# A Haar-wavelet convolution block on one core: a new order of VectorE's work in the head, moved steps around the last image, and GpSimd adding x for the first halves of five tail slots

## The chip, the cores and the metric

One NeuronCore of one Trainium2 chip runs the whole program. The metric is the device time of one execution in microseconds, median of several runs; lower is better.

## What is computed

For each of 8 images of 256 channels and 160x160 pixels, with all channels mixed by 1x1 convolutions:

```python
ll, lh, hl, hh = haar_dwt(x)                                   # 80x80 each
wav = concatenate([ll, lh, hl, hh], axis=1)                    # 1024 channels
fused = relu(bn_eval(conv1x1(wav, fusion_w, fusion_b), ...))   # 256 channels
sp_in = concatenate([mean(fused, 1), max(fused, 1)], axis=1)   # two maps
spatial_out = sigmoid(conv7x7(sp_in, sa_w)) * fused
ch_map = sigmoid(mlp(mean(spatial_out, (2, 3))) + mlp(max(spatial_out, (2, 3))))
projected = relu(bn_eval(conv1x1(ch_map * spatial_out, proj_w, proj_b), ...))   # 1024 channels
return haar_idwt(projected) + x
```

So an image's projection can't start before its fusion is complete, its two maps are convolved, the sigmoid has gated all of it, and the pooled channels have gone through the small network.

## The kernel before

**Tiles and slots.** An image is cut into 14 tiles of 6 or 5 rows of the 80x80 grid (480 or 400 pixels; 6,6,6,6,6,5,5 twice), 112 tiles in all. The program is a row of 133 slots. Slot k runs stage A (fusion) for tile k, while there is one, and stage C (projection, inverse Haar, add x, store) for tile kc = k - 21. Slots 0 to 20 have only A (the head), slots 112 to 132 only C (the tail). In the code `s.a` and `s.c` say which stages a slot has, `s.kn` is the next slot's kc, and `s.phase` is the slot's place (0 to 7) in what an image needs between its last fusion tile and its first projection tile:

- phase 0: the per-pixel sums and maxima over channels, collected in `blocksum` and `blockmax`, are turned by four TensorE transposes (`across_psum`), reduced by VectorE (`spatial_maps`) and sent through DRAM (`map_scratch`) to `maps`.
- phase 1: TensorE convolves (`convolve`, 28 matmuls), ScalarE takes the sigmoid, SP stores it (`sig_scratch`).
- phases 2 to 5: VectorE multiplies two chunks of 800 pixels a slot into `fused` (`gate`, four instructions at L896, `GATED`). The factors come by DMA, chunk by chunk, alternately into `sigb` and a piece of `xre`; for the last image all of them come in two DMAs into `x_lo` and `x_hi`. In the next slot ScalarE sums the same chunks (`chunk_means`).
- phase 6 (`LAST - 1`): VectorE pools (`pool_chunks`), TensorE multiplies by `squeeze`; phase 7 (`LAST`): `excite_channels`, the factors `ch`, and the first tile of C.

Slots 14 to 21 are phases 0 to 7 of the first image, slots 112 to 119 those of the last.

**Stage A of one tile** has two halves i (128 channels each). For each half: DMA to `xin`; ScalarE rounds to `x_hi` (`x_upper`, L633) once TensorE has read the previous tile's half; VectorE takes the rest, `x_lo = xin - x_hi` (`x_lower`, L777); TensorE runs 24 matmuls (`fusion`, L570). After both halves ScalarE writes `fused` (L725). For each tile GpSimd adds the two channel halves (`channel_sum`, L447) and VectorE takes their maximum, transposes both and reduces (`turn`, L913, L927, L932). In slots 1 to 11 VectorE also builds the matrices of the 7x7 convolution (`bands`, L832, L836).

**Stage C of one tile**: ScalarE and VectorE/GpSimd split y into `y_hi` and `y_lo` (L902 on VectorE, `lower` L462 on GpSimd), TensorE runs 24 matmuls for each half (`project`, L542), ScalarE and VectorE take relu and butterflies (L666, L861, L863), and VectorE writes the output pixels (`cells`, L880). x is added in one of two ways, which `adding(kc, i)` chooses: true, the cells go to `xre` and GpSimd issues a DMA that adds x from DRAM to them (L454); false, SP loads x to `xre` (`load_residual`, L351), the cells go to `xin`, and GpSimd adds them with four TENSOR_TENSORs (`sum_x`, L472). SP then stores `xre`.

**What sets the order.** Each engine's queue is written out by hand: `body(s)` of every engine is called slot after slot, and the engines meet in semaphores. What is written behind a waiting instruction on its engine waits too. SP is the queue of nearly all loads and stores.

In the head VectorE's `body` is, in this order: `x_lower(k+1, 0)`, `x_lower(k+1, 1)` (from slot 3 on), `turn`, first chunk's `gate`, `spatial_maps`, `bands`, second chunk's `gate`.

Of the kernel before, what the change touches and what calls it, by code (L numbers as in the profile page):

```python
# [11 lines left out]
P = 128  # L12
# [31 lines left out]
def haar_block(nc, x, fusion_w, fusion_b, bn1_g, bn1_b, bn1_m, bn1_v, sa_w, ca_w1, ca_w2,  # L44
# [47 lines left out]
    with ExitStack() as ctx:  # L92
# [191 lines left out]
        def adding(kc, i):  # L284

            return kc + LAG < NT or 2 <= kc + LAG - NT < LAST
# [33 lines left out]
        def _(sp):  # L320
# [46 lines left out]

            def store_sig(s):
# [4 lines left out]
            def body(s):  # L373
# [53 lines left out]
        def _(gp):  # L427
# [10 lines left out]
            def channel_sum(s):  # L438
# [5 lines left out]
                if s.load_next:  # L444
                    gp.wait_ge(xlo_ready[0], s.k + 2)
# [54 lines left out]
        def _(pe):  # L500
# [85 lines left out]

            def body(s):
                if s.a:
                    fusion(s, 0)
                if s.phase == LAST and not s.a:  # L590
                    excite_channels(s)
# [7 lines left out]
                if s.phase == 0:  # L599
                    pe.wait_ge(mlp_ready, 2)  # L600
                    pe.wait_ge(blockmax_ready, s.k)
                    pe.wait_ge(blocksum_ready, s.k)
                    for to, blocks in ((across_sum, blocksum), (across, blockmax)):
                        for h in range(2):
                            n = NPX // GROUP // 2
                            mm = pe.transpose(to[:, h * P:(h + 1) * P], blocks[:, h * n:(h + 1) * n], ident[:, :])
                    mm.then_inc(across_psum, 1)
# [5 lines left out]
                if s.c:  # L613
                    project(s, 1)
                if s.phase == 1 and not s.a:
                    convolve(s)
                if s.phase == LAST - 1:
                    pe.wait_ge(pool_ready, 2 * (s.nb + 1))
                    for i in range(CT):
                        mm = pe.matmul(squeezed, squeeze[:, i, :], pool[:, i, :], start=(i == 0), stop=(i == CT - 1))  # L620
# [408 lines left out]
```

## Time and profile before

| | |
|---|---|
| median of 3 runs | 2400.68 us (2397.55 to 2400.82) |
| the profiled execution, its own time | 2394.07 us |
| its span in the trace | 2392.3 us |
| TensorE busy | 2303.3 us (96%) |
| VectorE busy | 2065.7 us (86%) |
| ScalarE busy | 1137.2 us (48%) |
| GpSimd busy | 584.9 us (24%) |

The busy shares are means over a head, a long middle and a tail that differ; the rows further down take them apart. In the rows PE is TensorE, DVE VectorE, ACT ScalarE, POOL GpSimd and SPq the DMA issues of SP's queue.

### The profile page before, as it was taken

How to read it: one execution, taken by the hardware profiler on the slowest of the kernel's cores; microseconds unless marked ns; L12 is line 12 of the kernel's file. 1: busy time of each engine (PE TensorE's matmuls, PEld its weight loads, DVE VectorE, ACT ScalarE, POOL GpSimd, SP SyncE). 2: the span in 40 equal slices, each digit the busy share in tenths (PEclk: the TensorE clock that was granted, in tenths of full speed). 3: DMA queues.
4: the chain of work that ended last, by engine and by line, in shares of the span. 5: the costliest groups of instructions: out<-in, count | busy, mean ns of one | idle time of the engine just before them, and what ended most of it. 6: DMA issues, size and time to landing. Idle time of an engine off the chain costs nothing. (4 is left out here: it accounts for less than half of the span.)

```text
span 2392.3 us, 30200 instructions
## 1 busy us (share of the span) xinstructions
PE 2303.3 (96%) x11109; PEld 2039.9 (85%) x11109; DVE 2065.7 (86%) x2571; ACT 1137.2 (48%) x1535; POOL 584.9 (24%) x549
## 2 busy tenths in 40 slices
PE   7998799999999999999999999999999999998897
PEld 6886689888898988989899898988889898886786
DVE  6885688898888988899888989889888898889899
ACT  4443544465444554455444564446544464434433
POOL 0110122122221221211222112212212112133698
PEclk9999899999999999999999999999999999999999
DMA  5454499999999999999999999999999999989998
GB/s 188 168 183 147 151 277 283 278 310 284 294 286 295 288 286 288 288 281 306 282 277 297 293 307 281 283 278 297 295 293 283 283 307 280 280 238 286 346 354 324
DMA packets 112759, 660.54 MB, mean 276 GB/s; under 512 B 17698, under 2 KB 18788, under 8 KB 112356
## 3 DMA queue, kind: packets, MB, share of 16 engines
q1 hardware_dynamic: 84964, 479.04, 51.8%
q0 software_dynamic: 27648, 179.58, 39.2%
q8 instruction: 87, 1.43, 0.2%
q14 instruction: 60, 0.49, 0.1%
HBM read 448.24 MB, written 210.33 MB: 275 GB/s over the span
## 5 line engine op out<-in xcount | busy, mean ns | idle before, releaser
L542 PE MATMUL pp<-y_hi,wp_hi 128*128 128x480 f32 (+1 forms) x1792 | 670.5, 374 | 24.8 <-DVE sd L863 11.7
L633 ACT ACTIVATE x_hi<-xin 128x1920 fp32r<-128x1920 f32 (+1 forms) x224 | 418.7, 1869 | 542.9 <-PE pfs L570 461.0
L542 PE MATMUL pp<-y_lo,wp_hi 128*128 128x480 f32 (+1 forms) x1792 | 666.1, 372 | 0.0
L542 PE MATMUL pp<-y_hi,wp_lo 128*128 128x480 f32 (+1 forms) x1792 | 664.1, 371 | 0.0
L777 DVE TENSOR_TENSOR x_lo<-xin,x_hi 128x1920 fp32r<-128x1920 f32 (+1 forms) x224 | 461.5, 2060 | 214.1 <-ACT x_hi L633 213.1
L570 PE MATMUL pfs<-x_hi,wf_hi 128*128 128x480 f32 (+1 forms) x1648 | 616.4, 374 | 13.7 <-DVE x_lo L777 13.3
L570 PE MATMUL pfs<-x_lo,wf_hi 128*128 128x480 f32 (+1 forms) x1648 | 614.3, 373 | 0.0
L570 PE MATMUL pfs<-x_hi,wf_lo 128*128 128x480 f32 (+1 forms) x1648 | 614.2, 373 | 0.0
L666 ACT ACTIVATE relu<-pp,t 128x480 f32<-128x480 f32 (+1 forms) x448 | 285.6, 639 | 351.6 <-PE pp L542 351.2
L880 DVE SCALAR_TENSOR_TENSOR xre<-sd,both 128x960 f32<-128x960 f32 (+1 forms) x364 | 410.2, 1169 | 6.1
L542 PEld LDWEIGHTS pp<-y_hi,wp_hi 128*128 128x128 f32 x1792 | 338.2, 189 | 76.0 <-DVE sd L863 15.5
L542 PEld LDWEIGHTS pp<-y_hi,wp_lo 128*128 128x128 f32 x1792 | 337.9, 189 | 40.7
L542 PEld LDWEIGHTS pp<-y_lo,wp_hi 128*128 128x128 f32 x1792 | 337.8, 189 | 38.5
L454 POOL DMA_DIRECT2D xre<-in_x_dram x192 | 170.0, 885 | 800.0 <-DVE xre L880 800.0
L570 PEld LDWEIGHTS pfs<-x_hi,wf_hi 128*128 128x128 f32 x1648 | 311.5, 189 | 53.7 <-DVE x_lo L777 15.4
L570 PEld LDWEIGHTS pfs<-x_hi,wf_lo 128*128 128x128 f32 x1648 | 312.0, 189 | 36.7
L570 PEld LDWEIGHTS pfs<-x_lo,wf_hi 128*128 128x128 f32 x1648 | 311.4, 189 | 36.6
L861 DVE SCALAR_TENSOR_TENSOR sd<-pp,nbias,relu 128x480 f32<-128x480 f32 (+1 forms) x406 | 278.9, 687 | 53.3 <-PE pp L542 30.0
L863 DVE SCALAR_TENSOR_TENSOR sd<-pp,nbias,relu 128x480 f32<-128x480 f32 (+1 forms) x406 | 277.7, 684 | 0.0
L447 POOL TENSOR_TENSOR xre<-fused 128x480 f32<-128x480 f32 (+2 forms) x112 | 136.2, 1216 | 511.8 <-issue 258.2
L725 ACT ACTIVATE fused<-pfs,t 128x480 f32<-128x480 f32 (+1 forms) x206 | 129.2, 643 | 256.9 <-PE pfs L570 256.9
L462 POOL TENSOR_TENSOR y_lo<-y_full,y_hi 128x480 fp32r<-128x480 f32 (+1 forms) x112 | 134.2, 1198 | 472.9 <-DVE x_lo L777 410.4
(105 smaller groups left out, 1595.5 us busy)
## 6 DMA issues: line engine op xcount, KB each, us to landing
xin<-in_x_dram SPq DMA_DIRECT2D x160, 960.0 KB, 7.8
out_dram<-xre SPq DMA_DIRECT2D x160, 960.0 KB, 7.5
xre<-in_x_dram POOLq DMA_DIRECT2D x136, 960.0 KB, 10.3
xin<-in_x_dram SPq DMA_DIRECT2D x64, 800.0 KB, 7.3
out_dram<-xre SPq DMA_DIRECT2D x63, 800.0 KB, 5.9
xre<-in_x_dram POOLq DMA_DIRECT2D x56, 800.0 KB, 9.5
xre<-in_x_dram SPq DMA_DIRECT2D x24, 960.0 KB, 7.0
sigb<-sig_scratch SPq DMA_DIRECT2D x28, 400.0 KB, 8.5
```

What stands on the lines that cost most here:

```text
L447: nc.gpsimd.tensor_tensor(stats[:, 0:n], fused[:, 0, here], fused[:, 1, here], ALU.add).then_inc(sm_ready, 1)
L454: nc.gpsimd.dma_start(xre[:, home[g], 0:4 * px_of(kc)], dram(x_v, kc, i), accum_op=ALU.add).then_inc(x_added[home[g]], 16)
L462: nc.gpsimd.tensor_tensor(y_lo[:, kc % 2, 1, 0:n_px], y_full[:, 0:n_px], y_hi[:, kc % 2, 1, 0:n_px].bitcast(F32), ALU.subtract).then_inc(l ...
L542: mm = pe.matmul(pp[j][:, 0:n_px], w[:, kt, cols], y[:, s.pc, kt, 0:n_px], start=(kt == 0 and m == 0), stop=(kt == CT - 1 and m == 2))
L570: mm = pe.matmul(bank(s.k, o)[:, 0:n_px].rearrange("p (y w) -> p y w", w=W2), w[:, i, q, o * P:(o + 1) * P], v[:, q % 2, :, q // 2, :], st ...
L633: nc.scalar.activation(halves(x_hi, i, k), pairs(i, k), ACT.Copy).then_inc(xhi_ready[i], 1)
L666: nc.scalar.activation(relu[:, n, 0:n_px], pp[j][:, 0:n_px], ACT.Relu, bias=bias2[:, j * CT + i:j * CT + i + 1]).then_inc(r_ready, 1)
L725: nc.scalar.activation(fused[:, o, ring(s.k)], bank(s.k, o)[:, 0:px_of(s.k)], ACT.Relu, bias=bias1[:, o:o + 1]).then_inc(f_ready, 1)
L777: nc.vector.tensor_tensor(halves(x_lo, i, k), pairs(i, k), halves(x_hi, i, k).bitcast(F32), ALU.subtract).then_inc(xlo_ready[i], 1)
L861: nc.vector.scalar_tensor_tensor(rows[:, :, 0, :], p, low, q, ALU.max, ALU.add).then_inc(sd_ready, 1)
L863: nc.vector.scalar_tensor_tensor(rows[:, :, 1, :], p, low, q, ALU.max, ALU.subtract).then_inc(sd_ready, 1)
L880: nc.vector.scalar_tensor_tensor(px[:, :, :, c], s0, both[:, c, i:i + 1], s1, ALU.add, op).then_inc(cell_ready, 1)
```

## The change

No arithmetic changes. (1) In all head slots VectorE runs `head_body`: `turn` first, then `x_lower(k+1, 0)`, pooling, both chunks' gates, `spatial_maps`, `bands`, and `x_lower(k+1, 1)` last. (2) GpSimd's `channel_sum` no longer waits for `x_lower` in the head. (3) In slot 112 the four transposes stand behind `project(s, 1)` instead of ahead of it, `spatial_maps` behind `cells(s, 1)`, and SP stores the maps behind a store and a load. (4) In slot 118 the two small matmul groups stand inside `project(s, 1)`, the small relu ahead of the half's last relu, and `lower` of the next tile ahead of `cells(s, 1)`. (5) `adding` is false for the first halves of slots 114 to 118: SP loads x and GpSimd adds it there.

```diff
-            return kc + LAG < NT or 2 <= kc + LAG - NT < LAST
+            return kc + LAG < NT or i == 1 and 2 <= kc + LAG - NT < LAST
...
-                if s.phase == 0:
-                    sp.wait_ge(across_ready, 2 * (s.nb + 1))
-                    for m in range(2):
-                        sp.dma_start(map_dram[m:m + 1, :].rearrange("o (h p j) -> (o p) h j", h=2, j=GROUP),
-                                     across_all[:, m, :, :]).then_inc(map_stored, 16)
+                if s.phase == 0 and s.a:
+                    store_maps(s)
...
                 if s.c_next and not adding(s.kn, 1):
                     load_residual(s.kn, 1)
+                if s.phase == 0 and not s.a:
+                    store_maps(s)
...
                 gp.wait_ge(f_ready, CT * (k + 1))
-                if s.load_next:
+                if s.load_next and s.c:
                     gp.wait_ge(xlo_ready[0], s.k + 2)
...
                 for n, j in enumerate((LH, LL, HH, HL)):
+                    if s.phase == LAST - 1 and not s.a and i == 1:
+                        if n == 2:
+                            squeeze_channels(s)
+                        if n == 3:
+                            excite_channels(s)
...
                 for n, j in enumerate((LH, HH)):
+                    if n == 1 and i == 1 and s.phase == LAST - 1 and not s.a:
+                        hidden(s)
...
+            def head_body(s):
+
+                if s.turn:
+                    turn(s)
+                x_lower(s.k + 1, 0)
+                if s.phase == LAST - 1:
+                    pool_chunks(s)
+                if s.phase in GATED:
+                    for hand in range(2):
+                        gate(s, GATED[s.phase][hand])
+                if s.phase == 0:
+                    spatial_maps(s)
+                bands(s)
+                x_lower(s.k + 1, 1)
+                if s.c_next:
+                    lower(s.kn)
...
-                if s.c:
-                    butterflies(s, 1)
-                    cells(s, 1)
-                bands(s)
+                butterflies(s, 1)
+                if s.phase == LAST - 1 and not s.a:
+                    lower(s.kn)
+                cells(s, 1)
+                if s.phase == 0 and not s.a:
+                    spatial_maps(s)
```

VectorE's queue in a head slot with gates (slot 17), before; `x_lo` rows are `x_lower`, ISA rows the gate's instructions and their accumulator reads:

```order
L777 TENSOR_TENSOR x_lo<-xin,x_hi 128x1920 x2
L913 TENSOR_TENSOR xre<-fused 128x480
L927 STREAM_TRANSPOSE sd<-xre 128x960
L932 TENSOR_REDUCE blocksum<-sd 128x15
L932 TENSOR_REDUCE blockmax<-sd 128x15
L896 ISA fused,part<-fused,sigb 128x800
L896 ISA part 128x1
L896 ISA fused,part<-fused,sigb 128x800
L896 ISA part 128x1
L896 ISA fused,part<-fused,xre 128x800
L896 ISA part 128x1
L896 ISA fused,part<-fused,xre 128x800
```

The same place in the changed kernel:

```order
L955 TENSOR_REDUCE blockmax<-sd 128x15
L800 TENSOR_TENSOR x_lo<-xin,x_hi 128x1920
L919 ISA fused,part<-fused,sigb 128x800
L919 ISA part 128x1
L919 ISA fused,part<-fused,sigb 128x800
L919 ISA part 128x1
L919 ISA fused,part<-fused,xre 128x800
L919 ISA part 128x1
L919 ISA fused,part<-fused,xre 128x800
L919 ISA part 128x1
L800 TENSOR_TENSOR x_lo<-xin,x_hi 128x1920
L936 TENSOR_TENSOR xre<-fused 128x480
```

Turn and gates (four instructions, each with a read) stood behind both `x_lo` of their slot; now the turn stands ahead of both, and the gates between the two.

SP's queue in slots 112 and 113, before (`xre<-in_x_dram` are `load_residual`, `out_dram<-xre` stores):

```order
L351 DMA xre<-in_x_dram 128x1920
L391 DMA map_scratch<-sigb 100x2x32 x2
L359 DMA out_dram<-xre 128x1920
L351 DMA xre<-in_x_dram 128x1920
L402 DMA maps<-map_scratch 80x2x80
L359 DMA out_dram<-xre 128x1920 x2
L371 DMA sig_scratch<-sig 80x80
```

And in the changed kernel:

```order
L352 DMA xre<-in_x_dram 128x1920
L360 DMA out_dram<-xre 128x1920
L352 DMA xre<-in_x_dram 128x1920
L372 DMA map_scratch<-sigb 100x2x32 x2
L408 DMA maps<-map_scratch 80x2x80
L360 DMA out_dram<-xre 128x1920
L352 DMA xre<-in_x_dram 128x1920
L360 DMA out_dram<-xre 128x1920
L378 DMA sig_scratch<-sig 80x80
```

The map stores moved behind one store and one load of 960 KB, and slot 113 has a load more, for slot 114's first half.

GpSimd's queue over slots 114 to 116, before (`xre<-in_x_dram` is the adding DMA):

```order
L462 TENSOR_TENSOR y_lo<-y_full,y_hi 128x480
L454 DMA xre<-in_x_dram 128x1920 x2
L462 TENSOR_TENSOR y_lo<-y_full,y_hi 128x480
L454 DMA xre<-in_x_dram 128x1920 x2
L462 TENSOR_TENSOR y_lo<-y_full,y_hi 128x400
```

And in the changed kernel:

```order
L468 TENSOR_TENSOR y_lo<-y_full,y_hi 128x480
L478 TENSOR_TENSOR xre<-xre,xin 128x480 x4
L460 DMA xre<-in_x_dram 128x1920
L468 TENSOR_TENSOR y_lo<-y_full,y_hi 128x480
L478 TENSOR_TENSOR xre<-xre,xin 128x480 x4
L460 DMA xre<-in_x_dram 128x1920
L468 TENSOR_TENSOR y_lo<-y_full,y_hi 128x400
```

In each slot one adding DMA became four tensor instructions, which stand behind the slot's `cells(s, 0)`, that is beside VectorE's `y_lo` and first gate chunk.

## Rows read from the trace of the kernel before

**Rows 1.** The page, its first line.

```profile
span 2392.3 us, 30200 instructions
```

**Rows 2.** Stretches: length, busy time and instructions of each engine, granted clock, DMA share, GB/s.

```profile
20.00:182.00 162.00, 154.43 (x735) 134.87 (x734) 127.49 (x202) 72.00 (x64) 18.94 (x14) 1.00 0.48 169
182.00:300.00 118.00, 92.61 (x427) 80.33 (x426) 71.34 (x87) 58.96 (x78) 11.58 (x10) 0.90 0.43 149
300.00:2120.00 1820.00, 1818.64 (x8855) 1620.92 (x8854) 1608.21 (x1924) 891.52 (x1200) 369.59 (x360) 1.00 0.98 288
...
2169.00:2229.00 60.00, 44.37 (x210) 36.98 (x209) 59.58 (x94) 32.39 (x64) 12.89 (x14) 0.98 1.03 285
```

**Rows 3.** TensorE's waits, 20 to 182.5 us: total, times, longest.

```profile
PE pp L570 <- DVE x_lo L777: 4.4, 4, 1.8
PE pfs L570 <- DVE x_lo L777: 3.0, 3, 1.8
```

**Rows 4.** TensorE's waits, 182.5 to 300 us.

```profile
PE pfs L570 <- DVE x_lo L777: 10.3, 2, 5.6
PE pm L606 <- DVE blockmax L932: 7.1, 1, 7.1
PE pm L620 <- DVE pool L950: 4.9, 1, 4.9
PE pp L570 <- DVE x_lo L777: 3.0, 1, 3.0
```

**Rows 5.** Timeline of VectorE, slot 2 to 3: start, duration.

```profile
58.19 0.65 DVE L913 TENSOR_TENSOR xre<-fused 128x480 f32<-128x480 f32 x1
...
61.27 0.76 DVE L832 TENSOR_SCALAR band<-relu 80x80 f32<-80x80 f32 x4
...
63.36 2.15 DVE L777 TENSOR_TENSOR x_lo<-xin,x_hi 128x1920 fp32r<-128x1920 f32 x1
```

**Rows 6.** Timeline of ScalarE and VectorE, gates of slot 16, start of 17.

```profile
223.85 0.84 ACT L677 ACTIVATE pm<-fused 128x800 f32<-128x800 f32 x1 [6.03 <-DVE part L896]
...
225.72 1.91 ACT L633 ACTIVATE x_hi<-xin 128x1920 fp32r<-128x1920 f32 x1
...
227.66 2.16 DVE L777 TENSOR_TENSOR x_lo<-xin,x_hi 128x1920 fp32r<-128x1920 f32 x1 [2.02 <-ACT x_hi L633]
```

**Rows 7.** Timeline of VectorE and GpSimd, slots 5 and 6.

```profile
85.07 3.67 DVE L777 TENSOR_TENSOR x_lo<-xin,x_hi 128x1600 fp32r<-128x1600 f32 x2
87.02 2.81 POOL L447 TENSOR_TENSOR xre<-fused 128x480 f32<-128x480 f32 x1 [9.71 <-DVE x_lo L777]
88.66 1.68 DVE L913 TENSOR_TENSOR xre<-fused 128x480 f32<-128x480 f32 x1
```

**Rows 8.** DMA issues, 205 to 300 us: KB, median us to landing.

```profile
sigb<-sig_scratch SPq DMA_DIRECT2D x4, 400.0 KB, 4.1
...
sig_scratch<-sig SPq DMA_DIRECT2D x1, 25.0 KB, 4.2
```

**Rows 9.** The page, DMA issues of the whole run.

```profile
sigb<-sig_scratch SPq DMA_DIRECT2D x28, 400.0 KB, 8.5
```

**Rows 10.** Timeline of SP's queue and TensorE, slots 112 and 113.

```profile
2135.82 0.64 PE L606 MATMUL pm<-ident,blocksum 128*100 128x128 f32 x2 [5.34 <-DVE blockmax L932]
...
2146.54 0.80 SPq L391 DMA_DIRECT2D map_scratch<-sigb  x2
...
2156.86 2.63 PE L583 MATMUL pm<-maps,band 80*80 80x80 f32 x28 [2.15 <-DMA maps<-map_scratch]
```

**Rows 11.** Groups of GpSimd's instructions, 2120 to 2393 us: busy, mean ns.

```profile
L472 POOL TENSOR_TENSOR xre<-xre,xin 128x480 f32<-128x480 f32 (+1 forms) x124 | 145.4, 1209 | 15.3 <-DVE xin L880 12.8 <-DMA xre<-in_x_dram 2.5
```

**Rows 12.** Timeline of VectorE and GpSimd, second gates of slot 116.

```profile
2205.88 0.98 DVE L896 CUSTOM_DVE_ANT_0 fused<-fused,x_hi 128x800 f32<-128x800 f32 x1
...
2206.28 1.48 POOL L462 TENSOR_TENSOR y_lo<-y_full,y_hi 128x400 fp32r<-128x400 f32 x1
```

**Rows 13.** Timeline of GpSimd and TensorE, slots 118 to 119.

```profile
2227.59 1.19 POOL L462 TENSOR_TENSOR y_lo<-y_full,y_hi 128x480 fp32r<-128x480 f32 x1 [2.63 <-ACT y_hi L693]
...
2229.36 0.77 PE L542 MATMUL pp<-y_hi,wp_hi 128*128 128x480 f32 x1 [4.02 <-DVE y_lo L902]
```

More of the change, by code:

```diff
@@ L366, in load_sig, with store_maps @@
                              ).then_inc(sigb_landed[c % 2], 16)
+            def store_maps(s):
+                sp.wait_ge(across_ready, 2 * (s.nb + 1))
+                for m in range(2):
+                    sp.dma_start(map_dram[m:m + 1, :].rearrange("o (h p j) -> (o p) h j", h=2, j=GROUP),
+                                 across_all[:, m, :, :]).then_inc(map_stored, 16)
             def store_sig(s):
@@ L585, in convolve, with gather, squeeze_channels @@
                 mm.then_inc(conv_psum, 1)
+            def gather(s):
+                pe.wait_ge(mlp_ready, 2)
+                pe.wait_ge(blockmax_ready, s.k)
+                pe.wait_ge(blocksum_ready, s.k)
+                for to, blocks in ((across_sum, blocksum), (across, blockmax)):
+                    for h in range(2):
+                        n = NPX // GROUP // 2
+                        mm = pe.transpose(to[:, h * P:(h + 1) * P], blocks[:, h * n:(h + 1) * n], ident[:, :])
+                mm.then_inc(across_psum, 1)
+            def squeeze_channels(s):
+                pe.wait_ge(pool_ready, 2 * (s.nb + 1))
+                for i in range(CT):
+                    mm = pe.matmul(squeezed, squeeze[:, i, :], pool[:, i, :], start=(i == 0), stop=(i == CT - 1))
+                mm.then_inc(hid_psum, 1)
             def body(s):
@@ L598, in body @@
                     fusion(s, 1)
[L599 to L607, printed above, removed]
+                if s.phase == 0 and s.a:
+                    gather(s)
                 if s.phase == 1 and s.a:
@@ L614, in body @@
                     project(s, 1)
+                if s.phase == 0 and not s.a:
+                    gather(s)
                 if s.phase == 1 and not s.a:
                     convolve(s)
[L617 to L620, printed above, removed]
-                    mm.then_inc(hid_psum, 1)
+                if s.phase == LAST - 1 and s.a:
+                    squeeze_channels(s)
             body(slots[0])
@@ L950, in pool_chunks @@
                 nc.vector.tensor_reduce(pool[:, :, 1], part[:, 1, :, :], AX.X, ALU.max).then_inc(pool_ready, 1)
+            def head_body(s):
[13 more added lines that the diff above has]
+                    lower(s.kn)
             def body(s):
-                ahead = s.phase == LAST
+                if not s.c:
+                    head_body(s)
+                    return
                 if s.load_next:
                     x_lower(s.k + 1, 0)
-                if s.load_next and other(s.k) != other(s.k + 1):
-                    x_lower(s.k + 1, 1)
-                if ahead and not s.a:
-                    lower(s.kc)
-                if s.c:
-                    butterflies(s, 0)
-                    if s.phase == 0:
-                        turn(s)
-                    if s.phase == LAST - 1:
-                        pool_chunks(s)
-                    cells(s, 0)
+                butterflies(s, 0)
+                if s.phase == 0:
+                    turn(s)
+                if s.phase == LAST - 1:
+                    pool_chunks(s)
+                cells(s, 0)
                 if s.c_next and not s.next_is_first:
                     lower(s.kn)
-                if s.phase == LAST - 1 and not s.c:
-                    pool_chunks(s)
-                if s.turn and not (s.phase == 0 and s.c):
+                if s.turn and s.phase != 0:
                     turn(s)
@@ L974, in body @@
                     gate(s, GATED[s.phase][0])
-                if s.load_next and other(s.k) == other(s.k + 1):
+                if s.load_next:
                     x_lower(s.k + 1, 1)
-                if s.phase == 0:
+                if s.phase == 0 and s.a:
                     spatial_maps(s)
@@ L980, in body @@
                     lower(s.kn)
-                if s.c:
-                    butterflies(s, 1)
-                    cells(s, 1)
-                bands(s)
+                butterflies(s, 1)
+                if s.phase == LAST - 1 and not s.a:
+                    lower(s.kn)
+                cells(s, 1)
+                if s.phase == 0 and not s.a:
+                    spatial_maps(s)
                 if s.phase in GATED:
```

10 lines of the change are left out of this document (5 added, 5 removed).

## The prediction

> **What bounds the kernel now.** I read three views: the stretches, TensorE's waits, and the timelines around those waits. From 300 to 2120 us TensorE is busy 1818.6 of 1820 us [rows 2]: nothing but less TensorE work helps there, the change leaves every queue of those slots as it is, and a gain in the head therefore passes through it in full. The idle time is at both ends. From 20 to 182 us TensorE waits 4.4 + 3.0 = 7.4 us in seven places for VectorE's `x_lo` [rows 3]. From 182.5 to 300 it waits 10.3 + 7.1 + 4.9 + 3.0 = 25.3 us, always for VectorE [rows 4], at a granted clock of 0.90 [rows 2]: part of that stretch ran at 1.2 GHz, after waits of 5 to 7 us. The middle takes 1818.6 / 8855 = 0.205 us for a TensorE instruction, the stretch 182 to 300 has 427 of them, so 88 us of work took 92.6: about 5 us more are the clock's. From 2169 to 2229 us (slots 114 to 118) VectorE is busy 59.6 of 60 us and TensorE 44.4 [rows 2]: VectorE is the bound there, and whatever delays it is paid in full.
>
> **Slots 1 to 13.** A 480-pixel half of fusion is 24 matmuls of about 0.216 us (0.205 scaled to 6 rows), 5.2 us; a 400-pixel half 4.3. Between two halves run ScalarE's `x_hi`, 1.9 us [rows 6], and VectorE's `x_lo`, 2.1 us [rows 5]: 4.1 us with the handovers, so a half has 1.1 us to spare. VectorE's turn takes 61.27 - 58.19 = 3.1 us and the matrices 63.36 - 61.27 = 2.1 [rows 5]. Before, both stand in one gap between two `x_lo`, 5.2 us where 3.1 are free and 1.1 to spare: 1 us of wait a slot, and the seven waits are this. After, each gap holds one of the two. The turn alone still meets GpSimd's `channel_sum`, which now asks for SBUF just as `x_lo` ends. How such a meeting goes is seen once: GpSimd's sum took 2.81 us beside two `x_lo`, and VectorE's maximum behind them 1.68 instead of the 0.65 of [rows 5], until GpSimd was done [rows 7]. I count the turn at 3.1 + 1.1 = 4.2 us. VectorE's slot is then 2 x 2.1 + 4.2 + 2.2 = 10.6 against TensorE's 10.4: 0.1 to 0.2 us of wait in ten slots, 1.3 in all, and in the two pairs of 400-pixel slots, where TensorE needs only 8.6, about 1 us each. Left 3.3, **gain 4.1** (bounds 2 and 7.4).
>
> **Slots 14 to 20.** The turn of tile 13 now stands ahead of the transposes' need, so the 7.1 us wait goes. What replaces the others I follow in time, 0 being the end of slot 14's fusion. Fusion 15 runs 0.7 to 11.1, the convolution (2.6 us, [rows 10]) to 13.7. The sigmoid's store is issued at 16 (ScalarE's `x_hi`, relus and sigmoid), lands 4.2 later, the gate rows 4.1 after that [rows 8]: 24.3. VectorE has slot 16's first `x_lo` done by 23, waits for the rows, gates two chunks (four instructions of 0.98 overlapping to 0.91, [rows 12]) to 28.0, lets GpSimd's sum pass (1.2, [rows 11]), and has the second `x_lo` at 31.3, where TensorE wanted it at 29.3: 2.0 us of wait. From there VectorE's slot is turn, `x_lo`, gates 3.7, `x_lo`, that is 3.1 to 4.2 + 2.1 + 3.7 + 2.1 = 11 to 12 us, against TensorE's 10.4 (slots 17 and 18) and 8.6 (19 and 20). It gives waits of 0.1 and 0.5 in slot 17 to 18, 0.8 and 2.4 in 19, 0.6 and 1.2 in 20, and 2.2 ahead of the pooled matmul, which comes at 71.9. Sum 9.8. The decisive point is what no longer happens: ScalarE's `x_hi` at 225.72 stood behind a chunk sum that had waited 6.03 us for a gate, VectorE's `x_lo` then waited 2.02 for `x_hi` [rows 6], and TensorE for that. Now the gates of a slot are done before ScalarE asks for them in the next. Waits 25.3 - 9.8 = 15.5, and with no wait above 2.4 us most of the clock's 5 us, I say 4: **gain 19.5** (bounds 12 and 25).
>
> **Slot 112.** TensorE's 5.34 us wait for `blockmax` goes, since the transposes stand behind `project(s, 1)`. But the wait behind it grows. The convolution waited for the maps until 2156.86, and SP issued their stores only at 2146.54 [rows 10], although the transposes came at 2135.82: SP's queue stood behind a store's landing, which this change does not touch. Now one store and one load of 960 KB go ahead of the map stores too. Issue time for both is 0.8 us; their bytes take 3.4 us each at the 285 GB/s of [rows 2], but they were ahead of the load of the maps before as well, so I take 1.1 us of them: **loss 1.9**. Bounds: a gain of 7.4 if both waits vanish (5.3 + 2.1), a loss of 7.6 if all bytes come on top.
>
> **Slots 114 to 117, GpSimd's adds.** Four adds of 1.21 us [rows 11] start as `cells(s, 0)` ends, beside `y_lo` and the first chunk's two gate instructions. DMA gets lighter (share 1.03), but VectorE is the bound, and no wait on a DMA stands there. By the pattern of [rows 7] VectorE's next two-input instruction goes first, then GpSimd's and VectorE's alternate: `y_lo`, add, gate, add, gate, and the last two adds lie beside the butterflies. So two adds are paid a slot: three 480-pixel slots x 2.4 and one of 400 pixels x 2.0 = **loss 9.3**. The bounds: 0, if a gate never waits for GpSimd (none was seen to; [rows 12] show only GpSimd's `y_lo` stretched to 1.48 beside a gate of the usual 0.98), and 4 x 4.84 = 19.4, if every add is paid. I take the value between, as [rows 7] is the nearest case of VectorE waiting.
>
> The Trainium skill (SBUF — State Buffer, Who interferes with whom) says that a VectorE instruction with two SBUF inputs and a GpSimd instruction that reads SBUF exclude each other for the whole instruction, whoever starts first. [Rows 7] and [rows 12] agree, one for each direction. By the page alone this term is the loss just given, by [rows 12] alone it could be 0; the sum above keeps its value without the page.
>
> **Slot 118.** Before, GpSimd's `y_lo` waited 2.63 us for ScalarE and TensorE restarted at 2229.36 after 4.02 us [rows 13]. The moved matmuls let ScalarE finish the channel factors some 2 us sooner, but GpSimd now has four 400-pixel adds (4.1 us) ahead of that `y_lo`, and TensorE needs both halves of y. The two cancel: loss 0.5. With a lighter DMA the first residual of slot 119 lands sooner, for a gain of 1.2 of GpSimd's wait (2.5, [rows 11]). **Gain 0.7** (bounds: gain 4.0, the whole wait; loss 4.8, the whole adds).
>
> **Sum.** -4.1 - 19.5 + 1.9 + 9.3 - 0.7 = -13.1. Span 2392.3 [rows 1] to 2379.2. Beside the span the profiled execution has 1.8 us, so 2381.0; it ran 6.6 us under the median of the three runs, and against that median the prediction is 2400.7 - 13.1 = **2387.6**. Its own range, with 5 us either way in the head and 4 in the tail, is 2381 to 2394.
>
> **Rivals.**
> A, the gates are not held up by GpSimd. Speaks for it: no gate of before is seen stretched; against: hardly any met a running GpSimd instruction first. Without the 9.3 it is 2378.3.
> B, every add is paid, because GpSimd wins each boundary, `y_lo` and second-chunk gates included: 10.1 more, 2397.7, no change. For it: VectorE has no slack at all; against: two adds lie beside butterflies and cells, which read PSUM.
> C, slower. In the head `x_lower(k+1, 1)` is now queued behind gates that wait for a DMA. If the gate rows land as in the middle of the run, 8.5 us [rows 9], and not 4.1, each of four slots pays 4.4 more, 17.6: 2405.2. It decides from a landing of about 7.4 us on (13.1 / 4 = 3.3 more). For it: VectorE keeps its order whatever is late, and TensorE has 1.1 us to spare; against: the head's DMA share is 0.43 [rows 2], and the landings of just these loads are the 4.1.
> D, slot 112 gives its 5.3 and 2.1 us after all: 2378.3 as well.
>
> **From these to the numbers.** Likeliest case 0.52, A or D or a head better than counted 0.24, B or a head worse than counted 0.17, C 0.07. What can be told from no change is 0.2%, 4.8 us: 2395.9 to 2405.5. The likeliest case and A, D lie below it, B and a weak head about there, C at its upper edge or over it. Faster 0.82, same 0.13, slower 0.05. The range 2376 to 2397 takes in A, D and most of B.
>
> **What the changed profile would show.** Right: no wait for `blockmax` near 182 us, waits before 182 us of 3 us in all, none over 3 us up to 300, granted clock there 0.97 or more, ScalarE's chunk sums waiting for no gate; in slot 112 a longer wait for the maps, 8 to 11 us; in slots 114 to 117 one or two gate instructions a slot at 2 us instead of 0.98, and those slots 2 us longer each. Wrong: gates at 0.98 throughout there (A), `y_lo` and four gates stretched (B), or `x_lo` late behind idle VectorE time that a gate load ends (C).

## The result and the profile after

The changed kernel takes **2374.66 us** (median of 4 runs, 2371.9 to 2376.96), the kernel before 2399.11 beside it: ratio 0.9899, interval 0.9882 to 0.9917. That is 24.4 us faster, where 13.1 were forecast, and 1.3 us below the low end of the range. Timed again on another occasion (e7) it was 2375.05 against 2398.44, ratio 0.9905 (0.989 to 0.992). The profiled execution took 2376.96 us, the slowest of its four; that of the kernel before had been faster than any of the runs beside it. So the two first traces differ by only 17.3 us, and further traces of both were taken (e7, e8, e13, e14).

The stretches of the changed kernel, columns as in [rows 2]:

```profile
20.00:182.00 162.00, 159.94 (x764) 139.94 (x763) 144.50 (x210) 75.27 (x67) 28.25 (x15) 1.00 0.50 175
182.00:300.00 118.00, 111.95 (x541) 96.03 (x540) 99.29 (x112) 69.21 (x90) 20.48 (x16) 1.00 0.67 216
300.00:2120.00 1820.00, 1814.78 (x8839) 1616.59 (x8837) 1608.38 (x1931) 890.98 (x1204) 379.31 (x367) 1.00 0.98 287
2120.00:2169.00 49.00, 33.68 (x140) 28.62 (x141) 34.71 (x44) 15.04 (x28) 25.76 (x19) 0.79 0.88 301
```

In the second row TensorE does 541 instructions in the time of 427 [rows 2], at a granted clock of 1.00 for 0.90. The middle is full as before. The fourth row holds about slots 113 to 115: at a granted clock of 0.79 the convolution's 28 matmuls take 4.02 us behind a wait of 8.79, where they took 2.63 behind 2.15 [rows 10]. TensorE's waits, 20 to 182.5 us (two rows) and 182.5 to 300 us (three):

```profile
PE pp L581 <- DVE x_lo L800: 1.1, 2, 0.8
PE pfs L581 <- DVE x_lo L800: 0.8, 1, 0.8
...
PE pp L581 <- DVE x_lo L800: 3.5, 3, 1.8
PE pfs L581 <- DVE x_lo L800: 1.8, 2, 1.6
PE pm L612 <- DVE pool L973: 0.4, 1, 0.4
```

That is 1.9 us for the 7.4 of [rows 3], and 5.7 for the 25.3 of [rows 4]; the wait for `blockmax` is gone. Now the tail. SP's queue and TensorE in slots 112 and 113, the places of [rows 10]:

```profile
2116.03 1.74 SPq L372 DMA_DIRECT2D map_scratch<-sigb  x2
2126.29 0.31 SPq L408 DMA_DIRECT2D maps<-map_scratch  x1
2128.12 2.16 PE L594 MATMUL pm<-maps,band 80*80 80x80 f32 x14 [8.79 <-DMA maps<-map_scratch]
```

VectorE and GpSimd in slots 114 and 116, then GpSimd and TensorE in slots 118 to 119 ([rows 12, 13]):

```profile
2144.36 1.68 DVE L919 CUSTOM_DVE_ANT_0 fused<-fused,x_lo 128x800 f32<-128x800 f32 x1 [1.44 <-DMA x_lo<-sig_scratch]
2145.97 1.97 DVE L919 CUSTOM_DVE_ANT_0 fused<-fused,x_lo 128x800 f32<-128x800 f32 x1
...
2175.77 0.63 DVE L925 SCALAR_TENSOR_TENSOR y_lo<-fused,ch,y_hi 128x400 fp32r<-128x400 f32 x1
2175.99 6.46 POOL L478 TENSOR_TENSOR xre<-xre,xin 128x480 f32<-128x480 f32 x4 [2.73 <-DVE xin L903]
2176.31 2.01 DVE L919 CUSTOM_DVE_ANT_0 fused<-fused,x_hi 128x800 f32<-128x800 f32 x1
2178.25 1.97 DVE L919 CUSTOM_DVE_ANT_0 fused<-fused,x_hi 128x800 f32<-128x800 f32 x1
...
2205.65 4.44 POOL L478 TENSOR_TENSOR xre<-xre,xin 128x400 f32<-128x400 f32 x4 [4.95 <-DVE xin L903]
2210.05 1.20 POOL L468 TENSOR_TENSOR y_lo<-y_full,y_hi 128x480 fp32r<-128x480 f32 x1
2211.35 0.74 PE L553 MATMUL pp<-y_hi,wp_hi 128*128 128x480 f32 x1 [4.28 <-issue]
```

Two gate instructions take 2.01 and 1.97 us instead of 0.98, the four adds 6.46 us instead of 4.8: each gate lets one add pass, and the last two adds end behind the gates, beside the butterflies. In slot 118 the four adds stand ahead of `y_lo`, and TensorE restarts right behind it.

### The profile page after: what moved, and what is told of

The parts are those of the page before. It is cut to its first block and busy times, and to the rows that moved or that the text cites. A ratio compares the mean times of both kernels' runs of the same rounds, so it can differ in the third digit from the quotient of the medians.

```text
span 2375.0 us, 30224 instructions
## 1 busy us (share of the span) xinstructions
PE 2303.4 (97%) x11109; PEld 2038.4 (86%) x11109; DVE 2090.2 (88%) x2571; ACT 1138.7 (48%) x1535; POOL 621.6 (26%) x564
## 5 line engine op out<-in xcount | busy, mean ns | idle before, releaser
L453 POOL TENSOR_TENSOR xre<-fused 128x480 f32<-128x480 f32 (+2 forms) x112 | 147.5, 1317 | 462.3 <-issue 249.0
## 6 DMA issues: line engine op xcount, KB each, us to landing
xre<-in_x_dram POOLq DMA_DIRECT2D x133, 960.0 KB, 10.2
```

The source lines that it names most:

```text
L453: nc.gpsimd.tensor_tensor(stats[:, 0:n], fused[:, 0, here], fused[:, 1, here], ALU.add).then_inc(sm_ready, 1)
```

## The experiments

Four marks cut the run, each the start of an instruction: **mark 23**, the first matmul of slot 23's projection (305.75 us in the first trace of before); **conv**, the first matmul of slot 113's convolution; **restart**, TensorE's first matmul in slot 119; and the end of the span. All times in us.

| run | median (before beside it) | mark 23 | conv less mark | restart less conv | span |
|---|---|---|---|---|---|
| before, first trace | 2400.68 | 305.75 | 1851.1 | 72.5 | 2392.3 |
| e8 before | 2399.36 (2398.44) | 309.44 | 1852.9 | 73.6 | 2399.0 |
| e13 before | one execution, 2396.77 (2398.71) | 307.04 | 1851.8 | 73.2 | 2394.7 |
| e14 before | one execution, 2408.07 (2398.71) | 307.59 | 1853.6 | 73.7 | 2405.1 |
| changed, first trace | 2374.66 (2399.11) | 273.99 | 1854.1 | 83.2 | 2375.0 |
| e7 changed | 2375.05 (2398.44) | 274.25 | 1852.7 | 83.6 | 2374.3 |
| e1 changed, no adds | 2365.43 (2397.97) | 274.49 | 1853.0 | 72.6 | 2365.5 |
| e2 before + adds | 2405.37 (2397.97) | 307.08 | 1849.5 | 81.8 | 2402.6 |
| e3 before + head | 2368.37 (2397.97) | 273.76 | 1856.1 | 74.5 | 2369.9 |
| e4 changed, slot 112 as before | 2372.33 (2397.97) | 275.09 | 1852.3 | 82.4 | 2372.8 |
| e5 head + slot 118 | 2366.16 (2398.44) | 273.74 | 1852.4 | 72.7 | 2364.8 |
| e6 e1 + maps stored first | 2367.38 (2398.44) | 275.48 | 1852.5 | 72.9 | 2367.1 |
| e9 e5, gates behind | 2374.46 (2398.06) | 282.18 | 1852.0 | 72.6 | 2369.2 |
| e10 e5, matrices behind | 2379.84 (2398.06) | 286.76 | 1848.7 | 74.2 | 2373.6 |
| e11 e5, short sum | 2358.44 (2398.06) | 268.00 | 1850.0 | 71.8 | 2355.3 |
| e12 changed, adds in halves | 2373.83 (2398.06) | 274.11 | 1853.7 | 80.2 | 2371.2 |
| e15 e5, sum after maximum | 2369.45 (2398.71) | 278.07 | 1852.0 | 72.8 | 2372.4 |
| e16 e15, turn split | 2363.25 (2398.71) | 273.01 | 1852.7 | 72.8 | 2364.4 |

**e1, the adds undone.**

```diff
-            return kc + LAG < NT or i == 1 and 2 <= kc + LAG - NT < LAST
+            return kc + LAG < NT or 2 <= kc + LAG - NT < LAST
```

> The changed kernel with part 5 undone: in slots 114 to 118 the first halves' x comes by the adding DMA again. My theory (two GpSimd adds are paid a slot, because a gate meets a running add): every gate instruction there is back at 0.98 us, the restart of TensorE in slot 119 comes 9 to 11 us earlier than in the changed kernel (2211.35 there), and the median is 9 to 11 us under the changed kernel's 2374.7, that is 2364 to 2366. Rival (the adds are not what costs; what I read as their price is the slower clock or the later slot 112): gates at 0.98, but the restart within 3 us of 2211 and the median 2372 or more. Second rival (with DMA busy there, the adding DMAs push other transfers late): gates at 0.98 and new waits on DMA of 5 us or more, median about 2370.

Measured 2365.43, ratio 0.9857 (0.9841 to 0.9872), 9.2 us under the changed kernel; the restart came 11.3 us earlier than in its first trace, 0.3 more than expected. The theory held: the gates are back at 0.98, and the second rival's new waits on DMA don't show. Slot 114's gates and the restart:

```profile
2142.26 0.98 DVE L919 CUSTOM_DVE_ANT_0 fused<-fused,x_lo 128x800 f32<-128x800 f32 x1
2143.17 0.99 DVE L919 CUSTOM_DVE_ANT_0 fused<-fused,x_lo 128x800 f32<-128x800 f32 x1
...
2200.08 0.77 PE L553 MATMUL pp<-y_hi,wp_hi 128*128 128x480 f32 x1 [2.72 <-DVE y_lo L925]
```

**e2, the adds alone** (the diff of e1 the other way, in the kernel before).

> The kernel before with part 5 alone: in slots 114 to 118 SP loads x for the first halves and GpSimd adds it. Theory: first-chunk gate instructions take 2.0 us (480-pixel slots) and 1.8 us (400) instead of 0.98, and the whole is 9 to 11 us slower than the kernel before, with no wait on a DMA in it. Rival (gates not held up): 0 to 1 us slower. Rival (the price arises only together with the later transposes of slot 112): under 4 us slower.

Measured 2405.37, ratio 1.0027 (1.0017 to 1.0038): 7.4 us slower, a little under the theory's 9 to 11. Gates of slots 115 to 117 took 2.01, 1.97, 2.00, 1.97, 1.83 and 1.80. One clause was wrong: there is a wait on a DMA.

```profile
2168.03 5.05 POOL L472 TENSOR_TENSOR xre<-xre,xin 128x480 f32<-128x480 f32 x4 [0.35 <-DVE xin L880]
2173.28 0.99 DVE L896 CUSTOM_DVE_ANT_0 fused<-fused,x_lo 128x800 f32<-128x800 f32 x1 [4.78 <-DMA x_lo<-sig_scratch]
2174.20 0.98 DVE L896 CUSTOM_DVE_ANT_0 fused<-fused,x_lo 128x800 f32<-128x800 f32 x1
```

Slot 114's gates wait for their factors, here so long that the adds are over before them; in the changed kernel it is 1.44 us, in e12 2.33. The new load of x for slot 114 stands on SP's queue ahead of the sigmoid's store. From the issue of that store to the load of the factors behind it are 4.2 to 5.6 us in the five traces with this load, and 1.5 to 4.2 in the 13 without it (under 2.6 in ten). That the load delays the factors is read from this; no run has the load without the adds, and in e4, with both, slot 114's gates don't wait.

**e3, the head alone**, in the kernel before (`head_body` as in the change).

```diff
-                if s.load_next:
+                if s.load_next and s.c:
                     gp.wait_ge(xlo_ready[0], s.k + 2)
...
+                if not s.c:
+                    head_body(s)
+                    return
```

> The kernel before with parts 1 and 2 alone, the new order of VectorE's queue in the head and GpSimd's sum without its wait. Theory: the first projection wait of slot 23 comes 30 to 33 us earlier than before (305.75 there), as in the changed kernel (273.99); everything behind it moves as a block, so the median is 30 to 34 us under the kernel before, and together with the 9 to 11 us of the adds and some 2 of slot 112 that makes the 24.4 of the whole change. Rival (the head's gain is the 23.6 of the prediction, and the profiled executions differ by chance): 22 to 26 us in the median, while the slot 23 mark stands at 280 or later.

Measured 2368.37, ratio 0.9871 (0.9854 to 0.9887): 29.6 us faster, mark 23 at 273.76. The rival's 22 to 26 is refuted, the theory's 30 to 34 missed by 0.4. This part alone beats the whole change.

**e4, slot 112 as before; e5, only head and slot 118; e6, part 3 without its later stores.** The core of e4's edit (the same for `gather` and `spatial_maps`):

```diff
-                if s.phase == 0 and s.a:
+                if s.phase == 0:
...
-                if s.phase == 0 and not s.a:
-                    store_maps(s)
```

> The changed kernel with part 3 undone: transposes ahead of project(s, 1), spatial_maps ahead of the cells, the maps' stores ahead of a store and a load. Theory: 1 to 2 us faster than the changed kernel (2372.5 to 2373.7), because TensorE's 5.3 us wait for blockmax comes back but the 8.8 us wait for the maps falls to about 2; the conv starts 1.5 us earlier. Rival (the move itself pays, the stores' place is all that costs): 1 to 3 us slower, the maps wait still over 5 us on top of the 5.3. Rival (no difference): within 1 us, conv start within 0.5 us of 2128.1.

> Head and slot 118 alone: the changed kernel without part 3 (slot 112) and without part 5 (adds). Theory, by addition of what the first runs showed (part 3 costs 2.3 us, the adds 9.2): 2362 to 2364, that is 4 to 6 us under the head alone (2368.4), and TensorE's restart in slot 119 waits 2.7 us instead of 4.8. Rival (part 3 is worth what the difference between e3 and e1 shows, 2.9 us, and slot 118 nothing): 2368 or more.

> The changed kernel without part 5, and with SP's stores of the maps put back ahead of the store and the load in slot 112; the transposes stay behind project(s, 1) and spatial_maps behind the cells. Theory (the landing of small stores behind 960 KB transfers is what part 3 costs): stores are issued about 2115.1 and land about 5.4 us later, not 10; the maps are there 10.3 us after the issue as in the kernel before; the convolution starts at 2125 to 2126 instead of 2127.5 in e1, its wait is 6 to 7 us instead of 8.9, the median 1.5 to 3 us under e1's 2365.4. Rival (the maps share the DMA with the same bytes wherever they stand): conv at 2127 or later, within 1 us of e1.

e4: 2372.33, ratio 0.9887 (0.9872 to 0.9903), some 2.5 us under the changed kernel, 0.2 more than expected. Its waits are those of the theory, 5.34 us for `blockmax` and 2.56 for the maps, though conv comes 0.7 us earlier and not 1.5. But e5 at 2366.16 (ratio 0.9866, 0.9851 to 0.988) isn't below e1, and e6 at 2367.38 (0.9873, 0.9858 to 0.9887) isn't either: both expectations missed, by 2 us or more. The column conv less mark shows why nothing can be told by so little: the traces with the transposes ahead scatter from 1848.7 to 1856.1 there, with waits for the maps from nothing to 7.85 us. In the mean the 13 of them have 1851.9, and the four with the whole of part 3 (both of the changed kernel, e1, e12) 1853.4. e5 is also e3 with part 4: the restart's wait falls from 4.79 to 2.72 us as expected, restart less conv by 1.8, the median by 2.2. The stores in e6, for the three rows above of the changed kernel:

```profile
2116.82 0.80 SPq L372 DMA_DIRECT2D map_scratch<-sigb  x2
2122.37 0.32 SPq L406 DMA_DIRECT2D maps<-map_scratch  x1
2127.98 2.29 PE L592 MATMUL pm<-maps,band 80*80 80x80 f32 x15 [7.80 <-DMA maps<-map_scratch]
```

From issue to the load of the maps it is 5.5 us ahead of the two transfers and 10.3 behind them, as the theory says; but that load then takes 5.6 us instead of 1.8, so the place of 50 KB in the queue shifts the delay and saves 1 us of it. Part 3 costs 0 to 2.5 us by the medians, 1.4 by the means above.

**e7, e8, e13, e14: both kernels traced again,** unchanged.

> The changed kernel once more, so that it is timed on the same chip as these runs. Theory (the first comparison of it was fair, and the 7 us between the difference of the profiled executions, 17.3, and that of the medians, 24.4, come from the profiled execution of before being its fastest and that of the changed kernel its slowest): 23 to 25 us under the kernel before, 2373 to 2376. Rival (the medians were off): 17 to 20 us under it.

> The kernel before once more, with a new trace. Theory: the median is within 2 us of the runs beside it, and this trace, if it is of an execution near the median, shows where 5 to 6 us more are lost than in the first one: waits on DMA in the middle (300 to 2120 us, where the changed kernel has one of 1.04 us) or a lower granted clock at the two ends, 1 us or more each. Rival (nothing differs but the start): the mark of slot 23 within 1 us of 305.75 and the middle within 1 us of 1705.4.

> A third trace of the kernel before. Theory (its head varies by the granted clock behind the waits of 4 to 7 us, not by the waits): TensorE's waits from 182.5 to 300 us sum to 23 to 26 us again, while the slot 23 mark lies anywhere from 305.7 to 310 and goes with the clock of 182 to 300 us: about 306 at 0.90, about 309.5 at 0.84. Rival (the waits themselves vary): the mark over 308 with a clock of 0.90 and waits of 28 us or more.

> A fourth trace of the kernel before. The same expectation as for the third: the mark goes with the clock, not with the waits; over the four traces of before, the head's mean mark is 307 to 309, so that the head's gain is 33 to 35 us and not 31.8.

Mark 23 of the eight traces with the new head (the changed kernel, e1, e3 to e7, e12) lies between 273.7 and 275.5. With the old head it is 305.75, 309.44, 307.04 and 307.59, mean 307.5, as e14's expectation had it; e2, which has the old head too, lies at 307.08. e7's median is 23.4 us under the kernel before, as its theory says. (e14's span is long for another cause too: TensorE waits 5.0 us for `y_lo` at 2286.9, behind the restart, and from the restart to the end it takes 170.2 us where the other three take 162.7 to 163.1.) The stretch 182 to 300 of the old head in e8, e13 and e14:

```profile
182.00:300.00 118.00, 94.62 (x408) 82.57 (x408) 67.73 (x83) 57.67 (x76) 10.32 (x9) 0.84 0.45 149
```

```profile
182.00:300.00 118.00, 92.85 (x423) 80.28 (x422) 70.21 (x86) 58.34 (x77) 10.82 (x9) 0.88 0.44 149
```

```profile
182.00:300.00 118.00, 91.17 (x421) 79.04 (x420) 69.90 (x86) 58.33 (x77) 10.83 (x9) 0.90 0.45 149
```

e8's waits there sum to 23.3 us, less than the 25.3 of [rows 4], and yet its mark is 3.7 us later, with 408 instructions where [rows 2] have 427 and a clock of 0.84: matmuls at 1.2 GHz behind the waits of 4.5 to 7 us. e14 is the other kind: clock 0.90, waits of 26.7 us. So the expectation of e14 (only the clock varies) held for e8 and e13 and not for e14. In e8 the middle took what it took before (TensorE busy 1703.8 of the 1705 us from 310 to 2015, both times), so the waits on DMA there fall.

What the lower clock costs can be read without the waits. Up to mark 23 TensorE does the same 1206 instructions in every one of these traces (e14 records one fewer), so its busy time compares like with like: 259.08 us in the first trace of before, 264.88 in e8, 260.83 in e13, 259.65 in e14, but 252.30 and 252.05 in the two of the changed kernel. First before, then changed, columns as in [rows 2]:

```profile
0.00:305.75 305.75, 259.08 (x1206) 224.90 (x1206) 216.78 (x330) 140.37 (x152) 33.12 (x33) 0.96 0.48 167
...
0.00:273.99 273.99, 252.30 (x1206) 218.77 (x1206) 232.47 (x330) 141.21 (x152) 44.40 (x33) 1.00 0.54 186
```

**e9 and e10, the order inside the head.** In e5's `head_body` the gates, or the matrices, are put behind the second `x_lower`:

```diff
                 x_lower(s.k + 1, 0)
...
-                if s.phase in GATED:
-                    for hand in range(2):
-                        gate(s, GATED[s.phase][hand])
                 if s.phase == 0:
                     spatial_maps(s)
                 bands(s)
                 x_lower(s.k + 1, 1)
+                if s.phase in GATED:
+                    for hand in range(2):
+                        gate(s, GATED[s.phase][hand])
```

> e5 (head and slot 118) with one thing moved: in the head the gates of slots 16 to 19 stand behind x_lower(k+1, 1) instead of ahead of it; the turn stays first, the matrices stay between the x_lower. Theory (the gates' place between the two x_lo is what the gain of slots 14 to 20 rests on): 3.7 us of gates and 3.1 of turn lie in one gap between two x_lo, where 3.1 are free and 1.1 to spare, so 2.5 to 3.5 us of wait in each of four slots, ScalarE's chunk sums wait for gates again, and part of the stretch runs at the lower clock: the slot 23 mark 10 to 16 us later than the 273.7 of e5, the median 2376 to 2382. Rival (the turn's place is what mattered, since it alone took the 7.1 us wait away): the mark within 4 us of 273.7, median under 2370.

> e5 with one thing moved: in the head the matrices (bands) stand behind x_lower(k+1, 1) instead of ahead of it, so that they share a gap with the turn, as they did before the change. Theory (one wait a slot comes from two works in one gap): the waits of TensorE from 20 to 182 us are back at 7 to 9 us instead of 1.9, the slot 23 mark 5 to 8 us later than in e5, median 2371 to 2374. Rival (the gain before 182 us comes from GpSimd's sum no longer waiting for x_lo, and so reaching the turn early): waits stay under 4 us, median within 2 us of e5's 2366.2.

e9: 2374.46, ratio 0.9897 (0.9876 to 0.9919), 8.3 us slower than e5, its mark 8.4 later: below the theory's 10 to 16, above the rival's 4. The rest of the theory shows: ScalarE's chunk sums wait for gates again, 15.2 us in four places, and the granted clock from 182 to 300 us is 0.96. The gates' place is worth 8 us. e10: 2379.84, ratio 0.9925 (0.9906 to 0.9944), mark 13.0 us later where the theory had 5 to 8: its direction held, its size didn't. TensorE's waits, 182.5 to 300 us in e9, then 20 to 182.5 in e10:

```profile
PE pfs L579 <- DVE x_lo L796: 7.8, 2, 4.2
PE pm L610 <- DVE pool L969: 1.8, 1, 1.8
PE pp L579 <- DVE x_lo L796: 1.1, 1, 1.1
```

```profile
PE pp L579 <- DVE x_lo L796: 9.2, 6, 2.8
PE pfs L579 <- DVE x_lo L796: 2.8, 2, 1.9
```

12.0 us in e10 where before the change, with the same two works in one gap, 7.4 stood [rows 3]. The turn isn't longer: its maximum takes 0.65 us there. What GpSimd's sum, freed of its wait, now stretches is the matrices ahead of the turn, whose ten instructions took 2.2 to 2.3 us before:

```profile
112.38 3.17 DVE L855 SCALAR_TENSOR_TENSOR band<-relu,band 80x80 f32<-80x80 f32 x10
115.47 0.64 DVE L932 TENSOR_TENSOR xre<-fused 128x480 f32<-128x480 f32 x1
```

Before, the wait of part 2 kept the sum in VectorE's idle time: from 20 to 182 us the maximum took over 0.65 us twice only. So part 2 would cost something in the old order, and may cost it in the new one; it was never run by itself.

**e11, the short sum.**

```diff
-                nc.gpsimd.tensor_tensor(stats[:, 0:n], fused[:, 0, here], fused[:, 1, here], ALU.add
+                m = n if s.c or k == 0 else 40
+                near = ring_px(k // TILES, px, m)
+                nc.gpsimd.tensor_tensor(stats[:, 0:m], fused[:, 0, near], fused[:, 1, near], ALU.add
```

> e5 with GpSimd's channel_sum cut to 40 of its 480 or 400 columns in the head slots from 2 on (the map of sums is then wrong there; semaphores and all other work as in e5). It takes the meeting of this sum with VectorE out of the head. Theory (each head slot pays one meeting of about 1.0 us, on the maximum or on an x_lo, and TensorE has room for it but in the 400-pixel and the gated slots): the maximum takes 0.65 us instead of 1.68, no x_lo over 2.2 us; TensorE's waits from 20 to 300 us fall from 6.8 to 2 to 4; mark 3 to 5 us earlier, median 2361 to 2363. Rival (VectorE has slack there anyway): mark and median within 1 us of e5.

2358.44, ratio 0.9833 (0.9815 to 0.9851): mark 5.7 us earlier than e5's and the median 7.7 lower, both more than expected, TensorE's waits from 20 to 300 us 3.4. The meetings of the sum with VectorE cost the head 5.7 us. How they go, in the changed kernel, slots 15 and 16:

```profile
190.86 2.09 POOL L453 TENSOR_TENSOR xre<-fused 128x480 f32<-128x480 f32 x1 [8.84 <-ACT fused L748]
191.80 1.68 DVE L936 TENSOR_TENSOR xre<-fused 128x480 f32<-128x480 f32 x1
...
203.78 1.33 POOL L453 TENSOR_TENSOR xre<-fused 128x480 f32<-128x480 f32 x1 [10.82 <-ACT fused L748]
203.96 3.17 DVE L800 TENSOR_TENSOR x_lo<-xin,x_hi 128x1920 fp32r<-128x1920 f32 x1
207.05 0.64 DVE L936 TENSOR_TENSOR xre<-fused 128x480 f32<-128x480 f32 x1
```

Either the maximum takes 1.68 or an `x_lo` 3.17 with the maximum behind it at 0.64: one us for each sum, never both.

**e12, the adds in halves.**

```diff
-                for n in range(4):
-                    part_of = slice(n * px_of(kc), (n + 1) * px_of(kc))
+                cut = 2 if i == 0 and 2 <= kc + LAG - NT < LAST else 1
+                for n in range(4 * cut):
+                    part_of = slice(n * px_of(kc) // cut, (n + 1) * px_of(kc) // cut)
```

> The changed kernel with GpSimd's four adds for the first halves of slots 114 to 118 cut into eight of half the columns each; bytes and positions stay. Theory (a gate waits until the one GpSimd instruction that runs is over, and then goes first): a gate beside them takes 0.98 + 0.6 = 1.5 to 1.6 us instead of 2.0, the price of part 5 falls from 9.5 to about 5 us, median 2370 to 2371.5, TensorE's restart in slot 119 4 to 5 us earlier than 2210.5. Rival (GpSimd's run of adds is not broken into by instruction but VectorE gets a fixed share of the time): gates at 2.0 as before, median 2374 to 2376. Second rival (eight starts cost GpSimd more than the gates win): gates at 1.6 but GpSimd's string longer by 1.5 us or more and y_lo of the next tile late, median over 2375.

Slot 116 of e12:

```profile
2174.02 7.04 POOL L479 TENSOR_TENSOR xre<-xre,xin 128x240 f32<-128x240 f32 x8 [2.53 <-DVE xin L904]
2174.34 1.49 DVE L920 CUSTOM_DVE_ANT_0 fused<-fused,x_hi 128x800 f32<-128x800 f32 x1
2175.76 1.47 DVE L920 CUSTOM_DVE_ANT_0 fused<-fused,x_hi 128x800 f32<-128x800 f32 x1
```

The mechanism is as the theory has it: half an add, half the extra time of a gate. Restart less conv falls by 3.0 to 3.4 us; expected were 4 to 5. Slot 114's gates wait longer for their factors, 2.33 us, and so does the restart, 4.84 instead of 4.28. The median, 2373.83 (ratio 0.9896, 0.9881 to 0.9911), is 1.2 below e7's, too little to tell: the size was missed.

The Trainium skill (SBUF — State Buffer, Who interferes with whom) calls the port pair that VectorE and GpSimd share an exclusive lock, and says that the order of issue decides who blocks. The traces of e1, e2 and e12 agree, 0.98, 2.0 and 1.5 us; they add that a run of GpSimd instructions doesn't hold it, only one instruction at a time.

**e15 and e16, the place of the sum.** First the edit of e15, then what e16 adds:

```diff
+                if not s.c:
+                    gp.wait_ge(mx_ready, s.k)
...
+                if not s.c:
+                    maxima = slice(PXM, PXM + blocks * GROUP)
+                    nc.vector.transpose(to[:, maxima], stats[:, maxima])
+                    dve.wait_ge(sm_ready, s.k)
+                    both_maps = slice(0, PXM)
                 nc.vector.transpose(to[:, both_maps], stats[:, both_maps]).then_inc(stats_turned, 1)
```

> e5 with one wait added: in the head GpSimd's channel_sum starts when VectorE's maximum of the same tile is done. Theory (what is exclusive is exclusive wherever it stands: the transposes behind the maximum need the sum): the maximum takes 0.65 us and no x_lo more than 2.2, but VectorE waits 1.0 to 1.2 us for the sum in every turn, also in those where the sum ran beside an x_lo before; mark within 2 us of e5's 273.7, median 2365 to 2368. Rival (it is the collision with x_lo that costs): mark 2 to 5 us earlier, median 2361 to 2364.

> e15, and in the head the transposition of the turn is cut in two, the maxima's ahead of the wait for the sum, the sums' behind it. Theory (a transposition has one input and can lie beside GpSimd's sum of 1.1 us): the turn takes 0.65 + 1.1 + 0.65 + 0.65 + 0.6 = 3.6 us instead of the 4.2 of e5, so of the 5.7 us that e11 showed half come back: mark 2 to 4 us earlier than e5's 273.7 (269.7 to 271.7), median 2362 to 2364, the fastest that still computes everything. Rival (the transposition is held up by the sum too): the turn 4.2 us or more, no gain or a loss of up to 2 us.

e15: 2369.45 (0.9879, 0.9862 to 0.9897), mark 4.3 us later than e5, outside the theory's 2 and against the rival: VectorE waits 1.25 to 1.44 us for the sum in every turn, more than the 1.0 of a meeting. e16, first half of a turn:

```profile
205.69 0.65 DVE L934 TENSOR_TENSOR xre<-fused 128x480 f32<-128x480 f32 x1
206.38 0.68 DVE L951 STREAM_TRANSPOSE sd<-xre 128x480 f32<-128x480 f32 x1
206.51 1.23 POOL L453 TENSOR_TENSOR xre<-fused 128x480 f32<-128x480 f32 x1 [13.38 <-DVE xre L934]
207.78 0.68 DVE L954 STREAM_TRANSPOSE sd<-xre 128x480 f32<-128x480 f32 x1 [0.72 <-POOL xre L453]
```

The transposition beside the sum takes the same 0.68 us as the one alone, so one-input work does cover it. But 0.72 us of wait is left and the second instruction costs 0.2; mark 0.7 us earlier than e5, where 2 to 4 were expected, 2363.25 (0.9845, 0.9827 to 0.9863). It is the lowest median that still computes everything, but not by enough to tell it from e1 or e5.

## Why the prediction was wrong, step by step

The four marks, mean over four traces of before and two of the changed kernel: mark 23 -33.3 us, conv -32.3, restart -22.1, end -23.1. Forecast were -23.6, -21.7, -13.1 and -13.1. From mark 23 to the end 10.2 us are lost, where 10.5 were counted; so near a match is luck, as e14's late wait is in it. Without e14 the four read -33.3, -31.8, -21.5 and -20.7, and 12.6 us are lost. **The step that failed is the head**: 33.3 us of gain where 23.6 were counted, about 5 of the difference in the waits (9.8 left where 5.7 stayed, the largest piece) and 5 in the clock.

- **Slots 1 to 13** (4.1 forecast). 5.5 us of wait went. The turn at 4.2 us was right (the maximum takes 1.68), but no slot of 10.6 against 10.4 us waited 0.1 to 0.2: waits came in three places only, beside the 400-pixel slots.
- **Slots 14 to 20, waits** (15.5 forecast). 19.6 went. `blockmax` as said; slot 16 waited 1.41 for the 2.0 counted, slots 17 to 20 3.9 for 5.6, the pooled matmul 0.37 for 2.2. The prediction let the sum pass for 1.2 us ahead of slot 16's second `x_lo` and gave every later turn up to 4.2; the sum is met once, and a turn behind such an `x_lo` takes 3.1 (rows under e11). That this is why the later waits were counted too long is my reading, not a run's. The reading that ScalarE's chunk sums no longer stall held, and e9 prices the gates' place at 8 us.
- **The clock** (4 forecast). What the mark moved beyond the waits (20 to 300 us) is 31.8 - 5.5 - 19.6 = 6.7 us against the first trace; against e8 it is 35.4 - 5.1 - 17.6 = 12.7, against e13 8.7, e14 7.5: 8.9 in the mean. The busy time of the 1206 instructions says the same: 6.8, 12.6, 8.5 and 7.4 us over the changed kernel's first trace. I took 5 us from the stretch 182 to 300 of one trace and rounded down, and it was the trace that loses least by the clock. In the mean over the four the waits before 182 us gave 1.1 more than forecast, those behind it 3.9 and the clock 4.9: together the head's miss.
- **Slot 112** (loss 1.9). Wait 8.79 us, inside the 8 to 11 named; conv less mark rises by 1.1 in the mean of the two kernels' traces, by 1.4 over all runs. Rival D is false; the size is near the forecast, though medians don't show it (e4 against e5 and e6).
- **Slots 114 to 117** (loss 9.3). First chunks' gates 1.97 to 2.02 and 1.80 to 1.84 (slot 114's first, behind its wait, 1.68), second ones 0.98 to 0.99, `y_lo` as before: A and B are false, two adds are paid a slot. Each costs 1.0 us and not 1.2, so 2.0, 2.0 and 1.7 in slots 115 to 117, and 3.1 in slot 114, of which 1.44 are a wait that the prediction had excluded ("no wait on a DMA stands there"). That makes 8.8: the term is near the forecast since the two errors cancel.
- **Slot 118** (gain 0.7). Without the adds the restart's wait falls from 4.02 to 2.72 (e1, e5); with them it is 4.28, 0.3 over before, so a loss where a gain was counted. The adds cost 1.6 more here. 8.8 + 1.6 = 10.4 is the part's whole price at the restart (10.7 by the mean of restart less conv, changed kernel against e1, e5 and e6); e1's median says 9.2.
- **Rival C**: one gate of the head waited for its rows, 0.80 us, behind a landing of about 4 us; false.
- **Span to median.** Nothing in the sum covered that the first trace of before was 5.0 us under its median and that of the changed kernel 2.3 over its own. I had counted the shift as common to both.

The sign and most mechanisms were right, and the tail's sum came near with errors that cancel; the range was made around one trace, and the bound of the head (12 to 25 us for slots 14 to 20) took no spread of the clock in.

## What to carry to other kernels

Give each gap between two urgent instructions one piece of other work: here a new order of five calls on one engine, with part 2, moved mark 23 by 33 us (29.6 in e3's median), and two pieces in one gap (e9, e10) cost 8 and 13 of them. Count a GpSimd instruction with SBUF inputs as VectorE time where it meets VectorE work with two SBUF inputs, one instruction for each meeting, once, and put VectorE's one-input work beside it; GpSimd isn't free where VectorE is the bound. The old head, with waits of up to 7.1 us, kept TensorE busy for 259 to 265 us with the work that took 252 in the new one, so trace such a kernel more than once before sizing a gain.

## What the runs showed of the hardware

- Two stores of 25 KB took 5.5 us from issue to the load behind them where they were issued ahead of the next two transfers of 960 KB, and 10.3 behind them; the 50 KB load that followed took 5.6 and 1.8.
- A `STREAM_TRANSPOSE` beside a running GpSimd addition takes its usual 0.68 us, a gate with two SBUF inputs 2.0 instead of 0.98, and 1.5 when the addition is half as long.
- Four traces of the kernel before, with waits of 23.3 to 26.7 us from 182.5 to 300 us, had mark 23 anywhere over 3.7 us, at granted clocks from 0.84 to 0.90; eight traces with no wait over 1.8 us there kept within 1.8 us of each other.
